# Three splits and a copy change places in the queues of ScalarE and VectorE of a fused Perceiver layer

## The chip, the core and the metric

The kernel runs on one core of a Trainium2 chip. Its time is device microseconds (us) of one launch; the kernel before took 1712.28 us, the median of 3 runs (1712.24 to 1717.71). Lower is better. Five engines work side by side and each takes its own instructions strictly in order: TensorE (PE in the rows), VectorE (DVE), ScalarE (ACT), GpSimd (POOL) and SyncE (SP, which here issues the DMAs). They meet only at semaphores.

## The reference, cut to what matters

`x` is 256 x 512, the context `ctx` 25088 x 512. The layer is a cross attention of x over the context, then a self attention and a mixture of experts. The change touches the first part alone:

```
Q = layernorm(x);  q = Q Wq^T + bq;  k = ctx Wk^T + bk;  v = ctx Wv^T + bv      # 8 heads of 64
attn = softmax(q k^T / sqrt(64));  x = x + attn v
x = x + self_attention(layernorm(x));  x = x + experts(layernorm(x))
```

## The kernel before

The context is worked off in 49 chunks of 512 rows (NCH = 49). Matmuls run in float16; each float32 value is split into a high half, rounded to float16, and a low half, the rest, and a product takes three matmuls. Two operations belong to each split: ACT copies the value to float16 (the high half) and DVE or POOL subtracts that from the value (the low half).

K and V of a chunk are two groups (h = 0 is K, h = 1 is V) of seven block products each, a Strassen-like scheme: the units M1, M5, M6, M2, M7, M3, M4, 12 matmuls each (`unit`, L1067 to L1102). A unit reads the seven blocks of the split context, `ctx_s`: four blocks are the context itself, and the others are sums of blocks that POOL forms in `t_f`. Units add up in four half banks of `ps_proj`. The results are blocks C11, C22, C12 and C21; C11 lies in bank 0 for both K and V. ACT writes a block's high half (`block_highs`), DVE its low half (`block_lows`), and only after that the bank may be filled again. So M1, the first unit of each group, which starts bank 0 anew, waits for C11's low half of the group before it: `block_low` at least 4g - 3 (L1082). This is also the first unit of a step, and there it waits for the split context as well (L1080).

The work is a software pipeline over steps c (`cross_steps`). Step c does the softmax of chunk c, the projections of chunk c + 1 and the context split of chunk c + 2. A step has two halves, h = 0 and 1, and each half two of the four head pairs g = 2h and 2h + 1. For a head pair PE forms scores in `ps_s` (L1116); DVE takes their maximum (`maxima`, L777 and L784); ACT exponentiates (`exps`, L519, four instructions); ACT writes the high half of the probabilities (`p_highs`, L530) and DVE the low half (`p_lows`, L790); DMA turns them; PE multiplies them with V (L1134). `ps_s` holds one head pair, so the scores of the next wait for `exp_done`. DVE's `step_max` (L834) follows the maxima of a half's second head pair. `add_c22` (L825) completes C22, and the unit M4 waits for it (L1091).

The context split of chunk c + 2 lies in ACT's `ctx_highs` (L439 in half 0; L442 and twice L445 in half 1) and POOL's `ctx_parts` (L366 in half 0; L372 and twice L376 in half 1, the low halves). When POOL has done the last L376, `ctx_low` lets M1 of the next step start. Before half 0 POOL forms the block sums (L349 to L354), and `rescale` (L403 to L408) scales the running sums.

The order of each engine's queue is written out by hand in `step` of that engine; steps with all three chunks in range are c = 0 to 46.

Of the kernel before, what the change touches and what calls it, by code (L numbers as in the profile page):

```python
# [56 lines left out]
def exists(c, n, count=NCH):  # L57

    return not isinstance(c, int) or 0 <= c + n < count


def after(c, n, least=0):

    return not isinstance(c, int) or c + n >= least


def back(c, u, lag, per=NG):

    return (c, u - lag) if u >= lag else (c - 1, u - lag + per)


def layer(nc, x, ctxt, wq, wk, wv, bv, cols, w_in, wg, w1, w2, w3, out):
    with ExitStack() as ctx:
# [138 lines left out]
        def bank(h, role):  # L212

            return (0, (1, 2)[h], (2, 1)[h], 3)[role]

        def out_k(kk, odd, i, j):

            return k_s[odd][kk][:, 2 * i:2 * i + 2, j * HC:(j + 1) * HC]

        def out_v(kk, odd, i, j):  # L220

            return v_s[odd][kk][:, 2 * j:2 * j + 2, i * QUARTER:(i + 1) * QUARTER]


        C11, C22, C12, C21 = (0, 0, 0), (3, 1, 1), (2, 0, 1), (1, 1, 0)

        def half_bank(n):

            return ps_proj[:, n, :].rearrange("p (t k) -> p t k", t=2)
# [196 lines left out]
        def _(act):  # L426
# [8 lines left out]
            def ctx_highs(k, odd, half):  # L435

                if half == 0:
                    act.wait_ge(ctx_loaded[odd], 8 * k + (16 - 8 * odd))
                    act.activation(ctx_s[odd][0][:, 0:2, :, :].rearrange("p b t k -> p (b t) k"), ctx_f[odd][:, :, 0:QUARTER],  # L439
                                   ACT.Copy).then_inc(ctx_high, 1)  # L440
                else:
                    act.activation(ctx_s[odd][0][:, 2, :, :], ctx_f[odd][:, 2:4, QUARTER:CH], ACT.Copy).then_inc(ctx_high, 1)  # L442
                    for n in range(2):
                        act.wait_ge(t_sum, 4 * k + 3 + n)
                        act.activation(ctx_s[odd][0][:, 3 + 2 * n:5 + 2 * n, :, :], t_f[:, 2 * n:2 * n + 2, :, :],  # L445
                                       ACT.Copy).then_inc(t_high, 1)
# [17 lines left out]
            def seed(k, h):  # L464

                g = 2 * k + h
                act.wait_ge(unit_done, UNITS * g + 1)
                if not isinstance(k, int) or g >= 1:
                    act.wait_ge(block_low, 4 * g - 1)
                a, b = half_bank(bank(h, 0)), half_bank(bank(h, 1))  # L470
                if h == 0:
                    for t in range(2):
                        ins = act.activation(b[:, t, :], a[:, t, :], ACT.Identity, bias=bk_s[:, 2 + t:3 + t])
                else:
                    ins = act.activation(b, a, ACT.Copy)
                ins.then_inc(seeded, 1)
# [9 lines left out]
            def block_highs(k, h, which, odd):  # L486

                role, i, j = which
                g, ps = 2 * k + h, half_bank(bank(h, role))
                if which == C22:  # L490
                    act.wait_ge(c22_done, g + 1)
                else:
                    act.wait_ge(unit_done, UNITS * g + {C11: 4, C12: 6, C21: 7}[which])
                if h == 1:
                    ins = act.activation(out_v(0, odd, i, j), ps, ACT.Copy)  # L495
                elif which == C11:
                    for t in range(2):
                        ins = act.activation(out_k(0, odd, i, j)[:, t, :], ps[:, t, :], ACT.Identity, bias=bk_s[:, t:t + 1])
                else:
                    ins = act.activation(out_k(0, odd, i, j), ps, ACT.Copy)  # L500
                ins.then_inc(block_high, 1)
# [9 lines left out]
            def exps(c, g, odd):  # L511

                act.wait_ge(nmax_done, NG * c + g + 1)
                if g % 2 == 0 and after(c, -2):
                    act.wait_ge(scaled, 2 * (c - 2) + g // 2 + 1)
                for b in range(2):
                    for r in range(2):
                        col = 4 * g + 2 * b + r
                        ins = act.activation(prob[:, g % 2, (2 * b + r) * HC:(2 * b + r + 1) * HC],  # L519
                                             ps_s[:, b, r * HC:(r + 1) * HC], ACT.Exp, bias=nmax[odd][:, col:col + 1],  # L520
                                             scale=LOGIT_SCALE, accum_out=lsum[odd][:, col:col + 1])
                ins.then_inc(exp_done, 1)
# [9 lines left out]
            def step(c, odd):  # L532
                for h in range(2):
                    if exists(c, h):
                        block_highs(c + h, 1 - h, C21, odd if h == 0 else 1 - odd)
                    if exists(c, 1):
                        seed(c + 1, h)
                    pc, pg = back(c, 2 * h, 1)
                    if exists(pc, 0):
                        p_highs(pc, pg)  # L540
                    if exists(c, -1) and h == 0:
                        alphas(c - 1, 1)
                    if exists(c, 0) and h == 1:
                        alphas(c, 0)
                    if exists(c, 1):
                        copy_m5(c + 1, h)
                    if exists(c, 0):
                        exps(c, 2 * h, odd)
                    if exists(c, 0):
                        p_highs(c, 2 * h)  # L550
                    if exists(c, 1):
                        block_highs(c + 1, h, C11, 1 - odd)
                    if exists(c, 2):
                        ctx_highs(c + 2, odd, h)
                    if exists(c, 1):
                        for which in (C22, C12):
                            block_highs(c + 1, h, which, 1 - odd)
                    if exists(c, 0):
                        exps(c, 2 * h + 1, odd)
# [83 lines left out]
        def _(dve):  # L643
# [149 lines left out]
            def block_lows(k, h, which, odd):  # L793

                role, i, j = which
                g, ps = 2 * k + h, half_bank(bank(h, role))
                dve.wait_ge(block_high, 4 * g + 1 + (C11, C22, C12, C21).index(which))
                if h == 1:
                    ins = dve.tensor_tensor(out_v(1, odd, i, j), ps, out_v(0, odd, i, j), ALU.subtract)  # L799
                elif which == C11:  # L800
                    for t in range(2):
                        ins = dve.scalar_tensor_tensor(out=out_k(1, odd, i, j)[:, t, :], in0=ps[:, t, :], scalar=bk_s[:, t:t + 1],  # L802
                                                       in1=out_k(0, odd, i, j)[:, t, :], op0=ALU.add, op1=ALU.subtract)
                else:
                    ins = dve.tensor_tensor(out_k(1, odd, i, j), ps, out_k(0, odd, i, j), ALU.subtract)
                ins.then_inc(block_low, 1)
# [48 lines left out]
            def step(c, odd):  # L855
                for h in range(2):
                    if exists(c, h):
                        block_lows(c + h, 1 - h, C21, odd if h == 0 else 1 - odd)
                    if exists(c, 0):
                        maxima(c, 2 * h, odd)  # L860
                    if isinstance(c, int) and c == -1 and h == 1:
                        split_q()
                    pc, pg = back(c, 2 * h, 1)
                    if exists(pc, 0):
                        p_lows(pc, pg)
                    if exists(c, 1):
                        add_u4(c + 1, h)
                    if exists(c, -1):
                        add_o(c - 1, h)
                    if exists(c, 0):  # L870
                        p_lows(c, 2 * h)
                    if exists(c, 1):
                        add_c22(c + 1, h)
                        block_lows(c + 1, h, C11, 1 - odd)
                    if exists(c, 0):
                        maxima(c, 2 * h + 1, odd)
                        step_max(c, h, odd)
                    if exists(c, 1):
                        for which in (C22, C12):
                            block_lows(c + 1, h, which, 1 - odd)  # L880
                    if isinstance(c, int) and c == -1 and h == 1:
                        tisa_scores()

            cross_steps(dve, step)


# [413 lines left out]
```

## Time and profile before

| | |
|---|---|
| median of 3 runs | 1712.28 us |
| the profiled execution | 1712.28 us, of which the span is 1710.6 us |
| PE busy | 1566.7 us, 92% of the span |
| DVE busy | 1420.7 us, 83% |
| ACT busy | 1272.2 us, 74% |
| POOL busy | 792.5 us, 46% |
| chain that ended last, by engine | PE 32%, ACT 21%, DVE 19%, issue 15%, POOL 11% |

Busy is the time in which an engine has an instruction at work, of one execution. The chain is followed back from the last instruction, at each step to what released it. A share of busy time is an average over stages; the cross attention fills about 67 to 1365 us of the span, and there the steps repeat almost alike.

### The profile page before, as it was taken

The page shows a single profiled execution, that of the slowest core. Times are in us where ns is not written, and L with a number is a line of the kernel's source. Part 1 is how long each engine was busy: PE and PEld are TensorE (multiplying, and loading weights), DVE is VectorE, ACT ScalarE, POOL GpSimd, SP SyncE. Part 2 cuts the span into 40 slices and gives each one's busy share as a digit, 9 for nine tenths or more (in the row PEclk, how much of TensorE's full clock was granted, in tenths as well). Part 3 has the DMA queues.
Part 4 walks back from the last instruction along what each step waited for, and adds up shares of the span by engine and source line. Part 5 has one row for each costly group of instructions (what it writes and reads, how often), then busy time and mean ns, then how long its engine had stood idle before and what let it go on. Part 6 is the DMA issues. An engine that isn't in the chain of part 4 may idle for free.

```text
span 1710.6 us, 47409 instructions
## 1 busy us (share of the span) xinstructions
PE 1566.7 (92%) x17740; PEld 1273.3 (74%) x17740; DVE 1420.7 (83%) x1868; ACT 1272.2 (74%) x3075; POOL 792.5 (46%) x696
## 2 busy tenths in 40 slices
PE   3999999999999999999999999999999597999998
PEld 2777778777787787777877778778778365777776
DVE  8589888998888898988899888988988646776765
ACT  3588888888888888888888888888888534655554
POOL 5365665655656556566565565655654100000000
PEclk9999999999999999999999999999999675999999
DMA  4156445444454454544544445445455670455551
GB/s 166 45 106 137 121 102 133 107 126 123 104 140 102 120 131 102 135 122 101 134 106 125 124 103 141 101 119 132 104 134 112 149 234 1 151 219 187 212 191 50
DMA packets 442403, 216.03 MB, mean 126 GB/s; under 512 B 416736, under 2 KB 422880, under 8 KB 435568
## 3 DMA queue, kind: packets, MB, share of 16 engines
q1 hardware_dynamic: 442064, 215.07, 46.8%
q8 instruction: 34, 0.56, 0.1%
q10 hardware_dynamic: 288, 0.27, 0.1%
q14 instruction: 17, 0.14, 0.0%
HBM read 111.96 MB, written 0.56 MB: 66 GB/s over the span
## 4 chain that ended last, share of the span: by engine, by line
PE 32%; ACT 21%; DVE 19%; issue 15%; POOL 11%; DMA 1%; ACTq 0%; DVEq 0%; SPq 0%; POOLq 0%
ACT prob L519 14%; PE ps_proj L1099 10%; PE ps_proj L1234 9%; POOL ctx_s L376 8%; DVE cmax L777 8%; PE ps_o L1257 4%; DVE nmax L784 4%; PE ps_s L1116 4%; ACT p_s L530 3%; POOL ctx_s L372 3%; DVE k_s L802 2%; DVE ps_proj L825 2%; ACT ctx_s L442 2%; PE ps_s L1190 1%; PE ps_proj L1170 1%
## 5 line engine op out<-in xcount | busy, mean ns | idle before, releaser
L1099 PE MATMUL ps_proj<-ctx_s,wk_s 128*128 128x256 f16 x4116 | 496.8, 274 | 91.1 <-POOL ctx_s L376 65.2
L1099 PEld LDWEIGHTS ps_proj<-ctx_s,wk_s 128*128 128x128 f16 x4116 | 382.3, 98 | 175.9 <-issue 99.9
L1099 PE MATMUL ps_proj<-wv_s,ctx_s 128*128 128x256 f16 x4116 | 489.8, 273 | 0.0
L519 ACT ACTIVATE prob<-ps_s,nmax 128x256 f32<-128x256 f32 x784 | 360.3, 473 | 101.6 <-DVE nmax L784 101.0
L1099 PEld LDWEIGHTS ps_proj<-wv_s,ctx_s 128*128 128x128 f16 x4116 | 388.2, 98 | 62.8 <-issue 19.4
L790 DVE SCALAR_TENSOR_TENSOR p_s<-prob,p_s 128x1024 f16<-128x1024 f32 x196 | 243.7, 1243 | 80.7 <-ACT p_s L530 80.7
L777 DVE TENSOR_REDUCE cmax<-ps_s 128x4 f32<-128x1024 f32 x196 | 238.6, 1217 | 36.6 <-PE ps_s L1116 36.6
L372 POOL TENSOR_TENSOR ctx_s<-ctx_f,ctx_s 128x512 f16<-128x512 f32 x48 | 57.3, 1193 | 380.1 <-ACT ctx_s L442 380.1
L530 ACT ACTIVATE p_s<-prob 128x1024 f16<-128x1024 f32 x196 | 207.5, 1059 | 6.6
L376 POOL TENSOR_TENSOR ctx_s<-t_f,ctx_s 128x1024 f16<-128x1024 f32 x96 | 202.0, 2123 | 0.0
L1234 PE MATMUL ps_proj<-x_s,wsp 128*128 128x256 f16 x1536 | 179.9, 274 | 4.2 <-issue 3.2
L1134 PE MATMUL ps_o<-v_s,pt_s 128*128 128x64 f16 x4704 | 172.2, 194 | 8.5 <-DMA pt_s<-p_s 8.4
L1116 PE MATMUL ps_s<-k_s,q_s 64*128 64x256 f16 x2352 | 164.3, 273 | 15.5 <-ACT prob L519 15.5
L1234 PEld LDWEIGHTS ps_proj<-x_s,wsp 128*128 128x128 f16 x1536 | 151.0, 98 | 36.3 <-issue 3.5
L1134 PEld LDWEIGHTS ps_o<-v_s,pt_s 128*128 128x128 f16 x4704 | 166.1, 99 | 15.2 <-DMA pt_s<-p_s 10.7
L366 POOL TENSOR_TENSOR ctx_s<-ctx_f,ctx_s 128x1024 f16<-128x1024 f32 x48 | 102.1, 2127 | 134.0 <-ACT ctx_s L439 134.0
L519 ACT ACTIVATION_READ_ACCUMULATOR prob<-ps_s,nmax 128x1 f32 x784 | 160.8, 205 | 0.0
L1116 PEld LDWEIGHTS ps_s<-k_s,q_s 64*128 64x128 f16 x2352 | 99.3, 95 | 69.3 <-issue 30.5
L834 DVE TENSOR_TENSOR dmax<-nmax 128x8 f32<-128x8 f32 x98 | 143.3, 1462 | 3.4
L905 DVE SCALAR_TENSOR_TENSOR wsp<-wst,wsp 128x1024 f16<-128x1024 f32 x96 | 114.6, 1222 | 31.2 <-ACT wsp L585 31.2
L799 DVE TENSOR_TENSOR v_s<-ps_proj,v_s 128x512 f16<-128x512 f32 x196 | 125.4, 678 | 3.0 <-ACT v_s L495 3.0
L784 DVE SCALAR_TENSOR_TENSOR nmax<-cmax,nmax 128x4 f32<-128x4 f32 x196 | 106.2, 542 | 10.4
(156 smaller groups left out, 2016.4 us busy)
## 6 DMA issues: line engine op xcount, KB each, us to landing
ctx_f<-ctxt_dram SPq DMA_DIRECT2D x49, 1024.0 KB, 5.1
wst<-w_dram SPq DMA_DIRECT2D x96, 512.0 KB, 4.9
pt_s<-p_s SPq DMA_TRANSPOSE x392, 2.7
w_in_sb<-w_in_dram SPq DMA_DIRECT2D x1, 3072.0 KB, 10.9
tisa<-tisa_scores SPq DMA_DIRECT2D x3, 1024.0 KB, 14.5
w_f<-wk_dram SPq DMA_DIRECT2D x1, 1024.0 KB, 7.7
w_f<-wv_dram SPq DMA_DIRECT2D x1, 1024.0 KB, 11.5
w_f<-wq_dram SPq DMA_DIRECT2D x1, 1024.0 KB, 13.3
```

The source lines that it names most:

```text
L376: pool.tensor_tensor(out=low[:, 3 + 2 * n:5 + 2 * n, :, :], in0=t_f[:, 2 * n:2 * n + 2, :, :], in1=high[:, 3 + 2 * n:5 + 2 * n, :, :], op= ...
L519: ins = act.activation(prob[:, g % 2, (2 * b + r) * HC:(2 * b + r + 1) * HC], ps_s[:, b, r * HC:(r + 1) * HC], ACT.Exp, bias=nmax[odd][:, ...
L530: act.activation(p_s[:, g % 2, 0, :], prob[:, g % 2, :], ACT.Copy, scale=P_SCALE).then_inc(p_high, 1)
L777: dve.tensor_reduce(cmax[:, g % 2, :], ps_s[:, :, :].rearrange("p b (r k) -> p (b r) k", r=2), AX, ALU.max).then_inc(cmax_done, 1)
L784: dve.scalar_tensor_tensor(out=nmax[odd][:, 4 * g:4 * g + 4], in0=cmax[:, g % 2, :], scalar=-LOGIT_SCALE, in1=nmax[1 - odd][:, 4 * g:4 * g ...
L790: dve.scalar_tensor_tensor(out=p_s[:, g % 2, 1, :], in0=prob[:, g % 2, :], scalar=P_SCALE, in1=p_s[:, g % 2, 0, :], op0=ALU.mult, op1=ALU. ...
L799: ins = dve.tensor_tensor(out_v(1, odd, i, j), ps, out_v(0, odd, i, j), ALU.subtract)
L834: dve.tensor_tensor(dmax[:, cols], nmax[odd][:, cols], nmax[1 - odd][:, cols], ALU.subtract).then_inc(dmax_done, 1)
L1099: ins = pe.matmul(ps_proj[:, bank(h, role), sub * QUARTER:(sub + 1) * QUARTER], lhsT, rhs, start=(fresh and sub == 0 and t == 0 and i == 0 ...
L1116: ins = pe.matmul(ps_s[:, head, r * HC:(r + 1) * HC], q_s[a][rows, g, r * P:(r + 1) * P], k_s[odd][b][rows, g, r * HC:(r + 1) * HC], start ...
L1134: ins = pe.matmul(ps_o[:, vg // 2, col:col + DK], pt_s[:, vg, a, 4 * head + tile, :], v_s[vodd][b][:, tile, u * DK:(u + 1) * DK], start=(i ...
L1234: ins = pe.matmul(ps_proj[:, u % 2, m * T:(m + 1) * T], wsp[a][:, (u // 2) % 2, m, col:col + P], x_s[b][:, t, :], start=(t == 0 and k == 0 ...
```

## The change

In ACT's queue `ctx_highs` now comes directly behind the exponentials of the half's first head pair. Before, it stood behind that pair's `p_highs` and C11's high half; both come after it now. In DVE's queue the low half of C11 moves from behind `add_c22` to behind the maxima of the half's second head pair and `step_max`, where it leads C22 and C12. No instruction is added or removed; PE, POOL and SP keep their order.

```diff
@@ ACT, step(c, odd) @@
                     if exists(c, 0):
                         exps(c, 2 * h, odd)
+                    if exists(c, 2):
+                        ctx_highs(c + 2, odd, h)
                     if exists(c, 0):
                         p_highs(c, 2 * h)
                     if exists(c, 1):
-                        block_highs(c + 1, h, C11, 1 - odd)
-                    if exists(c, 2):
-                        ctx_highs(c + 2, odd, h)
-                    if exists(c, 1):
-                        for which in (C22, C12):
+                        for which in (C11, C22, C12):
                             block_highs(c + 1, h, which, 1 - odd)
                     if exists(c, 0):
                         exps(c, 2 * h + 1, odd)
@@ DVE, step(c, odd) @@
                     if exists(c, 1):
                         add_c22(c + 1, h)
-                        block_lows(c + 1, h, C11, 1 - odd)
                     if exists(c, 0):
                         maxima(c, 2 * h + 1, odd)
                         step_max(c, h, odd)
                     if exists(c, 1):
-                        for which in (C22, C12):
+                        for which in (C11, C22, C12):
                             block_lows(c + 1, h, which, 1 - odd)
```

DVE's queue in half 0 of a step before; L802 is the low half of C11 of K, L805 those of C22, C12 and, from the next half, C21:

```order
L790 SCALAR_TENSOR_TENSOR p_s<-prob,p_s 128x1024
L825 TENSOR_TENSOR ps_proj<-ps_proj,m_f 128x512
L802 SCALAR_TENSOR_TENSOR k_s<-ps_proj,bk_s,k_s 128x256 x2
L777 TENSOR_REDUCE cmax<-ps_s 128x4
L784 SCALAR_TENSOR_TENSOR nmax<-cmax,nmax 128x4
L834 TENSOR_TENSOR dmax<-nmax 128x8
L805 TENSOR_TENSOR k_s<-ps_proj,k_s 128x2x256 x3
```

And the same place of the changed kernel, whose lines stand two lower:

```order
L788 SCALAR_TENSOR_TENSOR p_s<-prob,p_s 128x1024
L823 TENSOR_TENSOR ps_proj<-ps_proj,m_f 128x512
L775 TENSOR_REDUCE cmax<-ps_s 128x4
L782 SCALAR_TENSOR_TENSOR nmax<-cmax,nmax 128x4
L832 TENSOR_TENSOR dmax<-nmax 128x8
L800 SCALAR_TENSOR_TENSOR k_s<-ps_proj,bk_s,k_s 128x256 x2
L803 TENSOR_TENSOR k_s<-ps_proj,k_s 128x2x256 x3
```

The pair for C11 moved behind three instructions. In half 1 it is the same with one instruction, L799, on V.

ACT's queue in half 1 of a step before, from the exponentials of head pair 2 to those of pair 3; L530 is `p_highs`, the first L495 the high half of C11 of V:

```order
L519 ACTIVATE prob,lsum<-ps_s,nmax 128x256 x4
L530 ACTIVATE p_s<-prob 128x1024
L495 ACTIVATE v_s<-ps_proj 128x2x256
L442 ACTIVATE ctx_s<-ctx_f 128x512
L445 ACTIVATE ctx_s<-t_f 128x1024 x2
L495 ACTIVATE v_s<-ps_proj 128x2x256 x2
L519 ACTIVATE prob,lsum<-ps_s,nmax 128x256 x4
```

And of the changed kernel:

```order
L519 ACTIVATE prob,lsum<-ps_s,nmax 128x256 x4
L442 ACTIVATE ctx_s<-ctx_f 128x512
L445 ACTIVATE ctx_s<-t_f 128x1024 x2
L530 ACTIVATE p_s<-prob 128x1024
L495 ACTIVATE v_s<-ps_proj 128x2x256 x3
L519 ACTIVATE prob,lsum<-ps_s,nmax 128x256 x4
```

The three context copies moved ahead of `p_highs`; in half 0 one copy, L439, did.

## Rows read from the trace of the kernel before

**Rows 1.** Waits, whole span: engine, line, releaser; us in total, times, longest

```profile
PE ps_proj L1099 <- POOL ctx_s L376: 65.2, 47, 1.4
```

**Rows 2.** Timeline, PE, one step; start, us, then idle before and its releaser

```profile
595.68 1.48 PE L1099 MATMUL ps_proj<-ctx_s,wk_s 128*128 128x256 f16 x12 [1.41 <-POOL ctx_s L376]
...
608.03 1.47 PE L1099 MATMUL ps_proj<-wv_s,ctx_s 128*128 128x256 f16 x12
609.68 0.83 PE L1116 MATMUL ps_s<-k_s,q_s 64*128 64x256 f16 x12 [0.17 <-ACT prob L519]
...
619.27 1.48 PE L1099 MATMUL ps_proj<-wv_s,ctx_s 128*128 128x256 f16 x12
622.14 1.48 PE L1099 MATMUL ps_proj<-ctx_s,wk_s 128*128 128x256 f16 x12 [1.40 <-POOL ctx_s L376]
```

**Rows 3.** Timeline, POOL, the same step

```profile
599.26 1.26 POOL L352 TENSOR_TENSOR t_f<-ctx_f,t_f 128x512 f32<-128x512 f32 x1
...
605.44 2.13 POOL L366 TENSOR_TENSOR ctx_s<-ctx_f,ctx_s 128x1024 f16<-128x1024 f32 x1 [2.63 <-ACT ctx_s L439]
...
607.69 1.04 POOL L405 TENSOR_TENSOR o_acc<-o_acc,alpha 128x512 f32<-128x512 f32 x1
...
616.63 1.20 POOL L372 TENSOR_TENSOR ctx_s<-ctx_f,ctx_s 128x512 f16<-128x512 f32 x1 [7.74 <-ACT ctx_s L442]
617.79 4.21 POOL L376 TENSOR_TENSOR ctx_s<-t_f,ctx_s 128x1024 f16<-128x1024 f32 x2
```

**Rows 4.** Timeline, ACT, the same step

```profile
604.31 1.05 ACT L439 ACTIVATE ctx_s<-ctx_f 128x1024 f16<-128x1024 f32 x1
...
612.46 0.47 ACT L519 ACTIVATE prob<-ps_s,nmax 128x256 f32<-128x256 f32 x1
...
614.49 1.06 ACT L530 ACTIVATE p_s<-prob 128x1024 f16<-128x1024 f32 x1
...
615.93 0.62 ACT L442 ACTIVATE ctx_s<-ctx_f 128x512 f16<-128x512 f32 x1
616.45 1.99 ACT L445 ACTIVATE ctx_s<-t_f 128x1024 f16<-128x1024 f32 x2
```

**Rows 5.** Timeline, DVE, the same step

```profile
599.31 1.23 DVE L784 SCALAR_TENSOR_TENSOR nmax<-cmax,nmax 128x4 f32<-128x4 f32 x1
...
604.86 0.69 DVE L825 TENSOR_TENSOR ps_proj<-ps_proj,m_f 128x512 f32<-128x512 f32 x1
605.47 0.87 DVE L802 SCALAR_TENSOR_TENSOR k_s<-ps_proj,bk_s,k_s 128x256 f16<-128x256 f32 x2
606.25 1.21 DVE L777 TENSOR_REDUCE cmax<-ps_s 128x4 f32<-128x1024 f32 x1
607.50 0.16 DVE L784 SCALAR_TENSOR_TENSOR nmax<-cmax,nmax 128x4 f32<-128x4 f32 x1
607.70 1.06 DVE L834 TENSOR_TENSOR dmax<-nmax 128x8 f32<-128x8 f32 x1
...
615.58 1.23 DVE L790 SCALAR_TENSOR_TENSOR p_s<-prob,p_s 128x1024 f16<-128x1024 f32 x1 [0.94 <-ACT p_s L530]
...
617.33 0.68 DVE L799 TENSOR_TENSOR v_s<-ps_proj,v_s 128x512 f16<-128x512 f32 x1
...
619.97 2.05 DVE L834 TENSOR_TENSOR dmax<-nmax 128x8 f32<-128x8 f32 x1
```

**Rows 6.** Timeline of the two first steps, DVE and POOL

```profile
78.59 0.17 DVE L834 TENSOR_TENSOR dmax<-nmax 128x8 f32<-128x8 f32 x1
...
96.53 2.37 DVE L790 SCALAR_TENSOR_TENSOR p_s<-prob,p_s 128x1024 f16<-128x1024 f32 x1
96.55 1.27 POOL L352 TENSOR_TENSOR t_f<-ctx_f,t_f 128x512 f32<-128x512 f32 x1
```

**Rows 7.** DMA issues of the page: kind, count, us to landing

```profile
pt_s<-p_s SPq DMA_TRANSPOSE x392, 2.7
```

**Rows 8.** Windows: us, busy (instructions) by engine, PE clock, DMA

```profile
600.00:1200.00 600.00, 565.27 (x7091) 471.32 (x7090) 537.36 (x683) 500.77 (x1272) 359.75 (x315) 1.00 0.48 120
```

## The prediction

> **What bounds the kernel now.** I read the waits over the whole span first, then one step of the timeline engine by engine; times "at s" are us from the start of the step's first unit M1 (595.68 in the trace). The reader is to see three things.
>
> First, PE is the engine at the limit, and one wait per step stands in its queue: 47 times it waits for POOL's last context low half, 65.2 us in all, about 1.4 us a time [rows 1]. The step from 595.68 to 622.14 lasts 26.46 us [rows 2]; 600 us of the loop hold 565 us of PE work at granted clock 1.00, that is 2.4 GHz [rows 8]. At most the 1.4 us wait and the 0.17 us before the third scores could come out of a step.
>
> Second, that wait is the end of a chain: ACT's L442, POOL's L372, twice L376, then M1 [rows 3, 4]. The exponentials that start at 612.46 give way to L530 at 614.49, and L442 starts only at 615.93: 1.44 us later, about what PE waits. Taking L442 ahead of the two operations is worth just the wait, if nothing else becomes late.
>
> Third, DVE and POOL shut each other out at times. The nmax at 599.31 works on 4 columns and took 1.23 us, ending with POOL's L352 [rows 3, 5], where the same instruction took 0.16 at 607.50; dmax took 1.06 beside L405 and 2.05 us beside the second L376, against 0.17 us at 78.59 [rows 3, 5, 6]. And one of the 1024-column `p_lows`, asked for as L352 ran (96.55 to 97.82), took 2.37 instead of 1.23: it ended 1.08 us after L352 [rows 5, 6]. I take it that a DVE instruction with two SBUF inputs waits for the POOL instruction that is running, and gets in before the next.
>
> **The change, half 0.** In its first part nothing moved. With M1 released later (below) POOL's sums lie about 1.7 us earlier against M1, so L352 (at s 3.6 to 4.8 before) is over when nmax is asked for at s 3.63; L354 behind it ends near 4.35. nmax ends at 4.4 instead of 4.86, the exponentials start at 4.45 and take 2.0. Then the moved copy L439 starts at 6.4 and holds ACT for 0.95, so `p_highs` starts at 7.35 and `p_lows` is asked for 1.1 us later (614.49 to 615.58 [rows 4, 5]), at 8.45. But POOL's L366 starts 1.13 us after L439 (604.31 to 605.44) and runs 2.13: 7.55 to 9.7. `p_lows` waits for it and ends 1.08 behind, at 10.75; before it ended at 9.27. So a copy of 1 us costs 1.5 us: 0.95 on ACT and 1.2 behind POOL, less the earlier exponentials.
>
> Behind it on DVE: `add_c22` 0.6 (604.86 to 605.47), maxima 1.25 (606.25 to 607.50), nmax 0.15: done at 12.7 [rows 5]. Before, C11's low half stood between, 0.8 us; now it comes next. `step_max` took 1.06 beside L405; POOL now does its L405 in the gap before, so I take 0.1, and then C11's low half, 0.87, ends at 13.7. M1 of the V group waits for exactly this half block and starts at 13.8, 0.1 behind its semaphore. Before it started at 12.35 (608.03 [rows 2]), right behind M4, since C11's low half had ended at 10.66 (605.47 + 0.87). A slack of 1.7 us has turned into a wait: +1.45 us. M4, held by `add_c22` to 11.4 instead of 11.04, is covered by this.
>
> **The change, half 1.** From M1 to the exponentials of head pair 2 took 4.43 us (608.03 to 612.46), 0.17 of it the scores' wait [rows 2, 4], which goes; so they start at 18.05, and end at 20.1 (2.03 us later). Now L442 and both L445 come first: L442 at 20.1, L445s from 20.6, `p_highs` at 22.5, `p_lows` asked for at 23.6. POOL's L372 starts 0.7 behind L442 at 20.8, lasts 1.1, and the first L376 runs from 21.9 to 24.0. `p_lows` falls into it, runs 24.0 to 25.1, and holds the second L376 off: 25.1 to 27.2. So the last context low half ends not 1.4 us earlier but 0.9 us later (26.32 before). `add_c22` ends at 25.7, so M4, which PE reaches 11.24 behind the group's M1 (608.03 to 619.27) at 25.0, waits 0.7; maxima end at 26.9, and nmax waits for the second L376, to 27.2. `step_max` falls beside `rescale`'s L405 as in half 0 before: 1.0. C11's low half 0.7 (617.33), semaphore 0.1: the next step's M1 starts at 29.0. Scores of head pair 0 follow M1 by 1.4 us, when the exponentials of pair 3 (27.25 to 29.3) are done. So the removed wait of 1.4 is replaced by two: about 1.1 us before M1 of V (M4 ends near 12.7) and about 1.9 before M1 of the next step (M4 ends near 27.1).
>
> **The rest.** `p_lows` of pair 0 comes 1.5 us later and of pair 2 about 4 us; their transposes land in 2.7 us [rows 7], and PE uses them two head pairs later (`PV_LAG`), where a head pair takes a quarter of a step, some 7 us: covered. The load of a context chunk follows the same `p_lows` on SP, again 1.5 us late, with most of a step to spare. C22's and C12's low halves come 1.3 us after C11's, before the seeds, which follow M1 (1.48 us [rows 2]), and M5, which comes after the scores, need their banks. If that cover were gone, they would add tenths per step.
>
> **The sum.** 29.0 - 26.46 = 2.54 us in each of 47 steps: 119 us. In step 47 no context is left to split; only half 0 is late, by 0.1 + 0.87 + 0.1 behind nmax, 0.7 us. The prologue step, where ACT writes a context copy ahead of C11's high half, may lose 1 us. Total +121. The profiled execution took 1712.28 us, the same as the median of the three runs, so the forecast is **1833 us**. My durations add overlaps of 0.05 to 0.1 at a dozen joints, so a step may lie anywhere from 28.3 to 29.4: 1800 to 1852 us.
>
> The Trainium skill bears on the third reading. SBUF — State Buffer, section "Who interferes with whom", says that VectorE's second input goes through a port shared with GpSimd, an exclusive lock for the whole instruction, and that an operation with one input in PSUM does not contend. By that rule all three collisions above block as the rows suggest, and C11's low half (one input in `ps_proj`) never does. One row of a `p_lows` held up is thin evidence for it; the rule lowers the chance of the first rival, and moves no term of the sum.
>
> **The rivals.** (1) *`p_lows` is not held by POOL.* For it: the 1.23 at 615.58 is the common size; against it: that one ran before L372, with POOL idle [rows 3, 5], and the one that met a running instruction took 2.37. Then `p_lows` ends at 9.65 in half 0, M1 of V starts at 12.7, and in half 1 `p_lows` runs 22.5 to 23.7, nmax ends at 25.7 to 26.2, depending on L405, and M1 starts at 26.6 to 27.2: +0.15 to +0.75 a step, 1719 to 1748 us.
> (2) *`p_lows` of pair 2 misses the gap.* It is asked for 0.4 us before the first L376 ends. If it comes behind that, it waits for the second, to 26.1, and ends at 27.2; `add_c22` 0.6, maxima 1.25, nmax 0.15, then dmax without L405 0.1, C11 0.7 and 0.1: M1 at 30.1, +3.6 a step, 1883 us.
> (3) *Faster: C11's low half gates nothing.* If the maxima and dmax on DVE run early enough that C11's low half ends before PE comes (within 12.35 and 25.0), the moved copies do what the chain says and the 65.2 us of waits go: 1647 us. It decides at 1.4 us of delay on DVE per half. For it speaks only that DVE idles 0.94 before `p_lows` [rows 5]; against it that nmax alone ended at 11.98 before (607.50 + 0.16), and C11's 0.87 behind it already makes 12.9.
> (4) *PE's clock.* The gaps grow from 1.4 to about 3.7 us a step. Granted clock was 1.00 with the present gaps [rows 8]; a fall to 1.2 GHz would put the time far above any case here. I give it 1 in 50.
>
> **How the numbers follow.** Forecast mechanism 0.69 (1800 to 1852), rival 1 0.10, rival 2 0.12, rival 3 0.05, rival 4 0.02, something of no effect 0.02. The range takes in half of rival 1's upper end, or a lock that acts in one place only, and the lower part of rival 2 in steps that now hit and now miss the gap: 1745 to 1875. Within 0.3% of 1712 us, which is about what can be told from no change, I put 0.04 (the lowest end of rival 1 and no effect), faster 0.06, slower 0.90.
>
> **What would show it.** PE's wait for L376 is gone or small, and PE waits for C11's low halves (L800 and L797 in the new file) before both M1, 1.1 and 1.9 us, and for `add_c22` before M4; `p_lows` averages about 1.6 us or more instead of 1.23, POOL's L376 about 2.6 instead of 2.1; dmax is short in half 0; the step lasts 29.0 us. It is wrong if `p_lows` stays at 1.23 beside POOL, if M1 starts at once, or if M1 waits for something else on DVE or ACT.

## The result: slower, by about a third of what was forecast

| | before | changed |
|---|---|---|
| median | 1714.99 us (4 runs) | 1758.26 us (4 runs) |
| profiled span | 1710.6 us | 1757.6 us |
| one step, M1 to M1 | 26.46 us | 27.37 us |

The ratio is 1.0247, 95% interval 1.022 to 1.0274: slower, and inside the range of 1745 to 1875 us, but 43 us where 121 were forecast, 119 of them in the steps. (The medians of before differ by 1 to 3 us between groups of runs; each ratio is taken against the runs beside it.)

The waits of the changed kernel over the whole span, with the columns of [rows 1]:

```profile
PE ps_proj L1096 <- DVE k_s L800: 40.5, 47, 0.9
PE ps_proj L1096 <- DVE v_s L797: 35.3, 47, 0.9
...
PE ps_proj L1096 <- DVE ps_proj L823: 26.9, 48, 1.3
```

The 47 waits for L376 are gone, as forecast, and in their place stand 47 waits for C11's low half of K, 47 for that of V, and 48 for `add_c22`. They sum to 102.7 us where 65.2 stood. These are the three waits that the prediction named; each is shorter than it said.

One step of PE, as in [rows 2]; it starts at 614.14 and the next at 641.51:

```profile
614.14 1.48 PE L1096 MATMUL ps_proj<-ctx_s,wk_s 128*128 128x256 f16 x12 [0.74 <-DVE v_s L797]
...
627.57 1.48 PE L1096 MATMUL ps_proj<-wv_s,ctx_s 128*128 128x256 f16 x12 [0.87 <-DVE k_s L800]
...
639.28 1.48 PE L1096 MATMUL ps_proj<-wv_s,ctx_s 128*128 128x256 f16 x12 [0.54 <-DVE ps_proj L823]
...
641.51 1.48 PE L1096 MATMUL ps_proj<-ctx_s,wk_s 128*128 128x256 f16 x12 [0.74 <-DVE v_s L797]
```

Its DVE, against [rows 5]; the first `p_lows` is that of pair 0, the second that of pair 2:

```profile
617.78 0.48 DVE L782 SCALAR_TENSOR_TENSOR nmax<-cmax,nmax 128x4 f32<-128x4 f32 x1
...
622.24 2.31 DVE L788 SCALAR_TENSOR_TENSOR p_s<-prob,p_s 128x1024 f16<-128x1024 f32 x1 [1.47 <-ACT p_s L530]
...
637.08 1.54 DVE L788 SCALAR_TENSOR_TENSOR p_s<-prob,p_s 128x1024 f16<-128x1024 f32 x1 [3.12 <-ACT p_s L530]
...
640.38 0.24 DVE L782 SCALAR_TENSOR_TENSOR nmax<-cmax,nmax 128x4 f32<-128x4 f32 x1
640.65 0.17 DVE L832 TENSOR_TENSOR dmax<-nmax 128x8 f32<-128x8 f32 x1
```

Its POOL, against [rows 3]:

```profile
616.97 1.27 POOL L352 TENSOR_TENSOR t_f<-ctx_f,t_f 128x512 f32<-128x512 f32 x1
...
621.34 2.13 POOL L366 TENSOR_TENSOR ctx_s<-ctx_f,ctx_s 128x1024 f16<-128x1024 f32 x1 [0.81 <-ACT ctx_s L439]
...
635.40 5.20 POOL L376 TENSOR_TENSOR ctx_s<-t_f,ctx_s 128x1024 f16<-128x1024 f32 x2
640.56 0.21 POOL L403 TENSOR_TENSOR l_acc<-l_acc,alpha 128x8 f32<-128x8 f32 x1
640.72 1.04 POOL L405 TENSOR_TENSOR o_acc<-o_acc,alpha 128x512 f32<-128x512 f32 x1
```

Both collisions are there. `p_lows` of pair 0 is asked for at 622.24, inside L366 (621.34 to 623.47), and ends at 624.55, 1.08 us behind it. `p_lows` of pair 2 is asked for at 637.08, inside the first L376, and the two L376 take 5.20 us where they took 4.21. But in the last row of DVE dmax took 0.17 us, where the prediction had priced it at 1.0.

And its ACT, against [rows 4]:

```profile
618.39 0.47 ACT L519 ACTIVATE prob<-ps_s,nmax 128x256 f32<-128x256 f32 x1
...
620.20 1.07 ACT L439 ACTIVATE ctx_s<-ctx_f 128x1024 f16<-128x1024 f32 x1
...
631.76 0.47 ACT L519 ACTIVATE prob<-ps_s,nmax 128x256 f32<-128x256 f32 x1
...
633.56 0.65 ACT L442 ACTIVATE ctx_s<-ctx_f 128x512 f16<-128x512 f32 x1
```

The copies start 1.81 and 1.80 us after the exponentials, not 2.0. What stood there before, `p_highs`, waits for the exponentials' semaphore and started 2.03 us after them in half 1 [rows 4] and 1.96 after them in half 0; the copies need nothing of them.

### The profile page after: what moved, and what is told of

Its sections match the earlier page's. It is cut to its first block, busy times and chain, and to the rows that moved or that the text cites. A ratio compares the mean times of both kernels' runs of the same rounds, so it can differ in the third digit from the quotient of the medians.

```text
span 1757.6 us, 47409 instructions
## 1 busy us (share of the span) xinstructions
PE 1581.0 (90%) x17740; PEld 1278.4 (73%) x17740; DVE 1311.5 (75%) x1868; ACT 1264.4 (72%) x3075; POOL 884.1 (50%) x696
## 4 chain that ended last, share of the span: by engine, by line
PE 36%; DVE 24%; ACT 21%; issue 16%; DMA 1%; DVEq 1%; ACTq 0%; POOL 0%; SPq 0%
PE ps_proj L1096 14%; ACT prob L519 10%; DVE cmax L775 9%; PE ps_proj L1231 9%; ACT p_s L530 6%; ACT ctx_s L445 4%; PE ps_s L1113 4%; PE ps_o L1254 4%; DVE ps_proj L823 4%; DVE nmax L782 2%; DVE v_s L797 2%; DVE k_s L800 2%; DVE p_s L788 2%; PE ps_s L1187 1%; PE ps_proj L1167 1%
## 5 line engine op out<-in xcount | busy, mean ns | idle before, releaser
L1096 PE MATMUL ps_proj<-wv_s,ctx_s 128*128 128x256 f16 x4116 | 491.9, 273 | 66.1 <-DVE k_s L800 40.5
L1096 PE MATMUL ps_proj<-ctx_s,wk_s 128*128 128x256 f16 x4116 | 494.6, 274 | 62.6 <-DVE v_s L797 35.3
L1096 PEld LDWEIGHTS ps_proj<-wv_s,ctx_s 128*128 128x128 f16 x4116 | 384.2, 98 | 147.0 <-DVE k_s L800 53.6
L788 DVE SCALAR_TENSOR_TENSOR p_s<-prob,p_s 128x1024 f16<-128x1024 f32 x196 | 305.1, 1557 | 224.6 <-ACT p_s L530 224.6
L372 POOL TENSOR_TENSOR ctx_s<-ctx_f,ctx_s 128x512 f16<-128x512 f32 x48 | 55.6, 1157 | 415.9 <-ACT ctx_s L442 415.9
L376 POOL TENSOR_TENSOR ctx_s<-t_f,ctx_s 128x1024 f16<-128x1024 f32 x96 | 248.6, 2613 | 0.0
L530 ACT ACTIVATE p_s<-prob 128x1024 f16<-128x1024 f32 x196 | 207.7, 1060 | 0.2
L1131 PE MATMUL ps_o<-v_s,pt_s 128*128 128x64 f16 x4704 | 172.6, 194 | 11.7 <-DMA pt_s<-p_s 11.7
L495 ACT ACTIVATE v_s<-ps_proj 128x512 f16<-128x512 f32 x196 | 113.1, 602 | 89.7 <-DVE ps_proj L823 83.7
L500 ACT ACTIVATE k_s<-ps_proj 128x512 f16<-128x512 f32 x147 | 83.2, 599 | 110.2 <-DVE ps_proj L823 108.7
L366 POOL TENSOR_TENSOR ctx_s<-ctx_f,ctx_s 128x1024 f16<-128x1024 f32 x48 | 103.3, 2152 | 49.6 <-ACT ctx_s L439 49.6
```

The source lines that it names most:

```text
L376: pool.tensor_tensor(out=low[:, 3 + 2 * n:5 + 2 * n, :, :], in0=t_f[:, 2 * n:2 * n + 2, :, :], in1=high[:, 3 + 2 * n:5 + 2 * n, :, :], op= ...
L530: act.activation(p_s[:, g % 2, 0, :], prob[:, g % 2, :], ACT.Copy, scale=P_SCALE).then_inc(p_high, 1)
L788: dve.scalar_tensor_tensor(out=p_s[:, g % 2, 1, :], in0=prob[:, g % 2, :], scalar=P_SCALE, in1=p_s[:, g % 2, 0, :], op0=ALU.mult, op1=ALU. ...
L1096: ins = pe.matmul(ps_proj[:, bank(h, role), sub * QUARTER:(sub + 1) * QUARTER], lhsT, rhs, start=(fresh and sub == 0 and t == 0 and i == 0 ...
L1131: ins = pe.matmul(ps_o[:, vg // 2, col:col + DK], pt_s[:, vg, a, 4 * head + tile, :], v_s[vodd][b][:, tile, u * DK:(u + 1) * DK], start=(i ...
```

## The experiments

The theory after the result: the forecast mechanism is right, and the step is 1.6 us shorter than forecast mainly because dmax in half 1 gets in before L405. The rivals: the two halves, or the two engines' parts, do something else than the prediction said, and 43 us is a chance sum. Each ratio below is against the kernel before, run beside it.

**VectorE's part alone.** Edit, on the kernel before:

```diff
                         add_c22(c + 1, h)
-                        block_lows(c + 1, h, C11, 1 - odd)
                     if exists(c, 0):
                         maxima(c, 2 * h + 1, odd)
                         step_max(c, h, odd)
                     if exists(c, 1):
-                        for which in (C22, C12):
+                        for which in (C11, C22, C12):
```

> VectorE's part of the change alone, ScalarE's queue as before. My theory (C11's low half behind the maxima and step_max makes both M1 wait): M1 of V starts 0.8 to 1.6 us later than the 12.35 us of before, and in half 1 dmax falls beside a context low half of GpSimd again, so that C11's low half ends behind it: 27.5 to 28.5 us a step against 26.46, about 1760 to 1806 us. Rival (the moved low halves hide, and the loss came from ScalarE's part): 1712 us, no wait for C11's low half before M1.

Measured: 1755.81 us, ratio 1.022 (1.019 to 1.025), just under the range given. Late low halves of C11 gate M1 without any help from ACT, so the rival falls. But the place was half right: only M1 of the next step waits, by 1.94 us, since dmax, held 2.05 us by the second L376, now stands ahead of C11's low half there; M1 of V shows no wait. Two of its steps on PE:

```profile
614.01 2.67 PE L1098 MATMUL ps_proj<-ctx_s,wk_s 128*128 128x256 f16 x12 [1.94 <-DVE v_s L799]
...
642.34 1.48 PE L1098 MATMUL ps_proj<-ctx_s,wk_s 128*128 128x256 f16 x12 [1.93 <-DVE v_s L799]
```

The plain step of this kernel lasts 26.87 us (642.34 to 669.21), +0.41. About every third step, as the one from 614.01, lasts 28.33: behind the wait the same 12 matmuls take 2.67 instead of 1.48 us, PE being at its lower clock level (granted 0.52 from 614 to 617 us, 1.00 from 642 to 645). 0.41 x 47 is 19 us of the 40 lost; the rest comes with the longer steps, 13 of them and the first.

**ScalarE's part alone.** Edit, on the kernel before:

```diff
+                    if exists(c, 2):
+                        ctx_highs(c + 2, odd, h)
                     if exists(c, 0):
                         p_highs(c, 2 * h)
                     if exists(c, 1):
-                        block_highs(c + 1, h, C11, 1 - odd)
-                    if exists(c, 2):
-                        ctx_highs(c + 2, odd, h)
-                    if exists(c, 1):
-                        for which in (C22, C12):
+                        for which in (C11, C22, C12):
```

> ScalarE's part of the change alone, VectorE's queue as before. My theory: p_lows comes 0.9 us later on ScalarE and is then held by GpSimd's L366 and by the first L376 (it averages about 1.55 us, not 1.22), M1 waits for no C11 low half, but the scores of the next pair wait for late exponentials: about 27.3 us a step, 1740 to 1775 us. Rival (the chain of the waits table is all that counts and VectorE's part did the harm): the 1.4 us wait is gone and the time is about 1650 to 1665 us.

Measured: 1833.65 us, ratio 1.0686 (1.0655 to 1.0716), far above the range. `p_lows` averages 1.56 us as expected, and no M1 waits for C11. The scores wait, in both halves:

```profile
604.34 0.83 PE L1114 MATMUL ps_s<-k_s,q_s 64*128 64x256 f16 x12 [1.27 <-ACT prob L519]
...
619.15 0.83 PE L1114 MATMUL ps_s<-k_s,q_s 64*128 64x256 f16 x12 [1.57 <-ACT prob L519]
```

The step is 29.0 us. With C11's low half ahead of the maxima, all that is late reaches nmax and the exponentials, and these are then the bound. So the two hunks do not add: 118 us for ACT's, 40 for DVE's, 43 for both. DVE's hunk takes C11's low half out of the softmax's chain, 0.8 us in half 0 and 0.6 in half 1, and with that pays back most of ACT's loss. The prediction left these times out of the chain in its sum, but named the hunk only as a cost and did not say what it gives.

**Half 0 alone, half 1 alone.** Edit, for half 0 on ACT; DVE is branched in the same way, and half 1 alone has the test turned round:

```diff
+                    if h == 0:    # the changed order
+                        ctx_highs(c + 2, odd, h)
+                        p_highs(c, 2 * h)
+                        for which in (C11, C22, C12):
+                            block_highs(c + 1, h, which, 1 - odd)
+                    else:         # the order of before
+                        p_highs(c, 2 * h)
+                        block_highs(c + 1, h, C11, 1 - odd)
+                        ctx_highs(c + 2, odd, h)
+                        for which in (C22, C12):
+                            block_highs(c + 1, h, which, 1 - odd)
```

> The whole change in half 0 only, half 1 as before. My theory: M1 of V starts 1.1 us later (13.4 instead of 12.35 us), the exponentials of pair 2 0.85 us later, and the wait for the context low halves stays at the end of the step: +0.85 us a step, 1752 us. Rival (half 1 is where the loss is made): 1712 us.

> The whole change in half 1 only, half 0 as before. In the changed kernel M1 of V to the next M1 took 13.94 us (613.43 minus 600.20 plus the rest of the step); behind a V group that starts at 12.35 as before this gives 26.3 us a step: 1700 to 1712 us, the gain of the earlier context split and the new wait for C11's low half cancel. Rival (half 1 carries the loss of the changed kernel): 1750 us or more.

Measured: half 0 alone 1789.44 us, ratio 1.0423 (1.0388 to 1.0458); half 1 alone 1702.58 us, ratio 0.9932 (0.9906 to 0.9958). The second is as expected, and faster than both kernels of the case: the loss is made in half 0. The first is 37 us above what I expected. Its step:

```profile
603.44 1.48 PE L1118 MATMUL ps_proj<-ctx_s,wk_s 128*128 128x256 f16 x12 [1.40 <-POOL ctx_s L376]
...
607.07 1.24 DVE L793 SCALAR_TENSOR_TENSOR nmax<-cmax,nmax 128x4 f32<-128x4 f32 x1
...
608.42 0.48 ACT L519 ACTIVATE prob<-ps_s,nmax 128x256 f32<-128x256 f32 x1 [0.69 <-DVE nmax L793]
...
617.60 1.48 PE L1118 MATMUL ps_proj<-wv_s,ctx_s 128*128 128x256 f16 x12 [0.86 <-DVE k_s L811]
```

Nmax of pair 0 took 1.24 us here, held by POOL, and the exponentials behind it start 4.98 us after M1, where in the changed kernel they start 4.25 after it (618.39 - 614.14). M1 of V follows at 14.16 (617.60 - 603.44) against 13.43 (627.57 - 614.14): the same 0.73. The wait of 1.40 for L376 stays, since half 1 has the old order. The step is 28.06 us. So in the changed kernel the late M1 of half 1 gives something back: POOL's sums have run further by then, and nmax of pair 0 waits only for the end of L352 (616.97 to 618.24) and takes 0.48 us. It is held there too, but for less. Half 0 costs +1.60 a step by itself, half 1 gives 0.22, and both together cost +0.91.

**A nudge ahead of dmax.** Edit, on the changed kernel: a wait for nmax and a one-column memset stand before dmax in half 1, so that dmax is asked for a little later.

```diff
                         maxima(c, 2 * h + 1, odd)
+                        if h == 1:
+                            dve.wait_ge(nmax_done, NG * c + 4)
+                            dve.memset(nudge[:, :], 0.0)
                         step_max(c, h, odd)
```

> The changed kernel with one tiny memset (one column) on VectorE between nmax and step_max's dmax in half 1. My theory of the miss: in half 1 dmax is asked for 0.07 us before GpSimd's L405 and so takes 0.17 us, where I had priced it at 1.0 behind L405; a tenth of a us more on VectorE lets L405 in first, dmax takes about 1.05, C11's low half and M1 come 0.85 us later: 28.2 us a step, about 1798 us. Rival (the order of asking is not what decides, or dmax is short for another reason): the memset costs its own 0.1 us, 1758 to 1765 us.

Measured: 1819.57 us, ratio 1.0617 (1.0599 to 1.0635); 61 us above the changed kernel and 22 above what I expected. DVE, POOL and PE about the end of one step; 613.18 is the next M1:

```profile
611.12 0.24 DVE L783 SCALAR_TENSOR_TENSOR nmax<-cmax,nmax 128x4 f32<-128x4 f32 x1
611.42 0.06 DVE L877 MEMSET nudge<- 128x1 f32 x1
611.47 1.05 DVE L833 TENSOR_TENSOR dmax<-nmax 128x8 f32<-128x8 f32 x1
...
611.47 1.04 POOL L406 TENSOR_TENSOR o_acc<-o_acc,alpha 128x512 f32<-128x512 f32 x1
...
613.18 1.48 PE L1100 MATMUL ps_proj<-ctx_s,wk_s 128*128 128x256 f16 x12 [1.68 <-DVE v_s L798]
...
616.41 1.26 POOL L355 TENSOR_TENSOR t_f<-t_f,ctx_f 128x512 f32<-128x512 f32 x1
...
616.82 0.88 DVE L783 SCALAR_TENSOR_TENSOR nmax<-cmax,nmax 128x4 f32<-128x4 f32 x1
```

In the changed kernel dmax is asked for at 640.65 and POOL's L405 at 640.72, and dmax takes 0.17. Here both are asked for at 611.47 and dmax takes 1.05. The step is 28.67 us, +1.30: 0.88 is dmax, and 0.38 is nmax of pair 0, which I had not expected to move: M1 is later against POOL's sums, so nmax now waits for the last of them (0.88 us) instead of for the end of the one before it (0.48), and the exponentials start at 4.63 after M1, not 4.25. 1.30 x 47 is 61. This is close to what the prediction described, 29.0 us and 1833, and it is one operation of eight columns that makes the difference.

**POOL's split behind `p_lows` in half 0.** Edit, on the changed kernel: POOL waits for `p_lows` of pair 0 before L366, which takes away the collision of half 0 and leaves all else.

```diff
                     pool.wait_ge(t_sum, 4 * k + 4)
+                    if after(k, -2):
+                        pool.wait_ge(p_low, NG * (k - 2) + 1)
                     pool.wait_ge(ctx_high, 2 * k + 1)
```

> The changed kernel, but GpSimd waits for the low half of head pair 0's probabilities before it starts L366. My theory (p_lows is held by the GpSimd instruction that runs): p_lows of pair 0 takes 1.22 again instead of 2.31 us, M1 of V comes 0.7 us earlier, about 26.6 us a step, 1720 to 1730 us; if dmax then falls behind L405 0.8 us of it are lost again (1758). Rival (the 2.31 us are a coincidence of something else): p_lows stays at 2.3 us and the wait adds to the time, 1758 us or more.

Measured: 1725.04 us, ratio 1.007 (1.0047 to 1.0093), as expected. The two operations that collided:

```profile
608.40 1.23 DVE L790 SCALAR_TENSOR_TENSOR p_s<-prob,p_s 128x1024 f16<-128x1024 f32 x1 [1.48 <-ACT p_s L532]
...
609.79 2.13 POOL L368 TENSOR_TENSOR ctx_s<-ctx_f,ctx_s 128x1024 f16<-128x1024 f32 x1 [3.11 <-DVE p_s L790]
```

`p_lows` takes 1.23 again, and M1 of V starts 12.74 us into the step instead of 13.43. 0.69 x 47 is 32, and 33 us are gone. So of the 43 us that the change costs, 33 hang on this one collision.

**Half 1 with the copies behind `p_highs`.** Edit, on the kernel before; half 0 is not touched.

```diff
                     # on ACT, half 1 (its if clauses left out)
                     p_highs(c, 2 * h)
-                    block_highs(c + 1, h, C11, 1 - odd)
                     ctx_highs(c + 2, odd, h)
-                    for which in (C22, C12):
+                    for which in (C11, C22, C12):
                         block_highs(c + 1, h, which, 1 - odd)
                     # on DVE, half 1
                     add_c22(c + 1, h)
-                    block_lows(c + 1, h, C11, 1 - odd)
                     maxima(c, 2 * h + 1, odd)
+                    block_lows(c + 1, h, C11, 1 - odd)
                     step_max(c, h, odd)
```

> From the kernel before, half 1 only: the context copies go ahead of C11's high half but stay behind p_highs, and C11's low half goes behind the maxima but ahead of step_max. Half 0 as before. My theory: L442 comes 0.47 us earlier, p_lows meets no GpSimd instruction, C11's low half ends before PE needs the bank (25.1), the wait for the context shrinks by 0.47: 26.0 us a step, 1690 us. Rival (the exponentials' chain decides by now): 1705 to 1715 us, with new waits of the scores for exponentials.

Measured: 1713.04 us, ratio 0.9996 (0.9987 to 1.0006): nothing, where 1690 was expected. A miss, and this is why (three engines, half 1):

```profile
618.26 0.61 ACT L442 ACTIVATE ctx_s<-ctx_f 128x512 f16<-128x512 f32 x1
...
618.39 1.23 DVE L799 SCALAR_TENSOR_TENSOR p_s<-prob,p_s 128x1024 f16<-128x1024 f32 x1 [0.94 <-ACT p_s L530]
...
618.95 1.68 POOL L372 TENSOR_TENSOR ctx_s<-ctx_f,ctx_s 128x512 f16<-128x512 f32 x1 [7.26 <-ACT ctx_s L442]
```

L372 is released earlier than before, but now inside `p_lows` (618.39 to 619.62), and takes 1.68 us instead of 1.20 [rows 3]. It ends 1.01 behind `p_lows`. The 0.47 us that ACT saved is lost on POOL, and M1 still waits 1.40 for L376. The collision works in both directions.

**L442 in half 0.** Edit, on the kernel just shown: L442, which needs only the context chunk, is moved from half 1 to half 0, ahead of the exponentials of pair 1.

```diff
-                else:
+                elif half == 2:
                     act.activation(ctx_s[odd][0][:, 2, :, :], ...)   # L442
+                else:
                     for n in range(2):                               # the L445s
...
+                    if exists(c, 2) and h == 0:
+                        ctx_highs(c + 2, odd, 2)
                     if exists(c, 0):
                         exps(c, 2 * h + 1, odd)
```

> As the last, and L442 moves into half 0, into the 0.87 us for which ScalarE waits before the exponentials of pair 1, so that GpSimd does L372 in its idle time and only the two L376 hang on ScalarE in half 1. My theory: the second L376 ends at about 25.4 us, M1 at 25.5: 25.5 us a step, about 1667 us. Rival (the scores then wait for the exponentials of pair 3, or nmax for the earlier L376): 1685 us or more.

Measured: 1663.68 us, ratio 0.9705 (0.9687 to 0.9723), as expected. The step is 25.37 us:

```profile
611.24 0.17 DVE L847 TENSOR_TENSOR dmax<-nmax 128x8 f32<-128x8 f32 x1
...
611.24 1.08 POOL L405 TENSOR_TENSOR o_acc<-o_acc,alpha 128x512 f32<-128x512 f32 x1
...
620.14 4.31 POOL L376 TENSOR_TENSOR ctx_s<-t_f,ctx_s 128x1024 f16<-128x1024 f32 x2 [6.55 <-ACT ctx_s L446]
...
622.17 0.20 DVE L797 SCALAR_TENSOR_TENSOR nmax<-cmax,nmax 128x4 f32<-128x4 f32 x1
...
624.61 1.48 PE L1125 MATMUL ps_proj<-ctx_s,wk_s 128*128 128x256 f16 x12 [0.31 <-POOL ctx_s L376]
```

L372 is out of half 1, the two L376 follow ACT's copy at once, and M1 waits 0.31 for them instead of 1.40. The two first rows bear on the nudge: dmax and L405 are asked for at the same 611.24, and here dmax got in. Between 300 and 1200 us the two starts of half 0 lie within 0.01 us of each other in 36 steps of this kernel; dmax took 0.17 us in 9 of them and 1.06 in the others. With half 1 alone it was 4 of 34, in the kernel before none of 34. Where dmax started 0.06 to 0.08 us ahead of L405, it took 0.17 every time, in every kernel here.

**The same with the first L445 early.** Edit, on top (cut to the call; `ctx_highs` is divided to match): the first of the two L445 goes behind `alphas` in half 1, ahead of the exponentials of pair 2.

```diff
                         alphas(c, 0)
+                    if exists(c, 2) and h == 1:
+                        ctx_highs(c + 2, odd, 3)     # L445 with n = 0
                     if exists(c, 1):
                         copy_m5(c + 1, h)
```

> As e8_l442_half0, and the first of the two L445 moves to behind alphas in half 1, so that GpSimd does the first L376 in its idle time too. My theory: the second L376 then ends near 23.8 us, well before PE is done with M4 (25.1): the last 0.31 us of wait for the context go, about 25.1 us a step, 1650 us. Rival (the exponentials of pair 2 come 0.6 us later for the copy, and scores then wait for exponentials): 1664 us or more.

Measured: 1627.45 us, ratio 0.9495 (0.9482 to 0.9508), better than expected and the fastest kernel of this study, by 5.05% against before. A window as in [rows 8], here from 300 to 1200 us:

```profile
300.00:1200.00 900.00, 900.00 (x11396) 761.78 (x11392) 776.62 (x1095) 800.83 (x2046) 586.79 (x513) 1.00 0.51 128
```

PE is busy 900.00 of 900.00 us and a step lasts 24.70 (609.64 to 634.34), the next 24.61: no engine makes it wait any more. Before, it waited 1.40 and 0.17 us a step, 1.57 together; the step is 1.76 to 1.85 shorter. The rest is busy time: before, PE was busy 846.60 of the same 900 us, 24.9 us a step. Why that shrank by 0.2 is not shown.

**L442 in half 0 alone.** Edit, on the kernel before: only the diff of "L442 in half 0".

> The kernel before with one edit: L442 moves into half 0, ahead of the exponentials of pair 1; every other instruction keeps its place. My theory (L372 on GpSimd, 1.2 us, is what the move takes off the end of the chain, and no p_lows is pushed beside a GpSimd instruction): the second L376 ends 0.7 us earlier, 25.75 us a step, about 1680 us. Rival (the rest of e8's edits carried its gain): 1705 us or more.

Measured: 1691.26 us, ratio 0.9871 (0.9851 to 0.9891); 11 us less gain than expected. The reason is again nmax:

```profile
606.41 4.21 POOL L376 TENSOR_TENSOR ctx_s<-t_f,ctx_s 128x1024 f16<-128x1024 f32 x2 [7.25 <-ACT ctx_s L446]
...
608.52 2.12 DVE L788 SCALAR_TENSOR_TENSOR nmax<-cmax,nmax 128x4 f32<-128x4 f32 x1
...
612.66 0.83 PE L1120 MATMUL ps_s<-k_s,q_s 64*128 64x256 f16 x12 [0.42 <-ACT prob L520]
```

Nmax is asked for at 608.52, when the first L376 has just given way to the second, and waits all of it: 2.12 us for four columns. In the kernel with both edits it takes 0.20, as it comes 0.07 before that point (622.17; the first of the pair takes about 2.10 and ends at 622.24). The exponentials of pair 3 start later for it, and the next scores wait 0.42 us for them. A step is 25.96 us where 25.75 was expected; 0.21 x 47 is 10 of the 11 us.

## Why the prediction was wrong in size and right in mechanism

The sign and the mechanism held; the size was off by a factor of 2.8. That 1758 us lies inside 1745 to 1875 is luck: the forecast mechanism was given 1800 to 1852, and the range had been widened downward for rival 1 or a lock that acts in one place only, neither of which came. Times from M1 of the step, of the changed kernel against the prediction:

| | forecast | measured |
|---|---|---|
| exponentials of pair 0 | 4.45 | 4.25 |
| L439 | 6.4 | 6.06 |
| `p_lows` of pair 0 ends | 10.75 | 10.41 |
| M1 of V | 13.8 | 13.43 |
| exponentials of pair 2 | 18.05 | 17.62 |
| L442 | 20.1 | 19.42 |
| `p_lows` of pair 2 ends | 25.1 | 24.48 |
| second L376 ends | 27.2 | 26.46 |
| dmax lasts | 1.0 | 0.17 |
| next M1 | 29.0 | 27.37 |

- **The step that failed** is "`step_max` falls beside `rescale`'s L405 as in half 0 before: 1.0". Before, dmax of half 0 was asked for at 607.70 and L405 at 607.69 [rows 3, 5], and it took 1.06. In the changed kernel it is asked for 0.07 us before L405 (0.06 to 0.08 in all steps between 300 and 1200 us) and takes 0.17. That is 0.83 of the 1.63 us by which the forecast step is too long. It has a consequence in the next half 0: M1 comes sooner after POOL's sums have begun, so nmax of pair 0 is held by L352 and not, as forecast, by L354, and the exponentials start at 4.25 instead of 4.45. The nudge shows both: asked for 0.11 us behind nmax instead of 0.03, dmax takes 1.05, the exponentials start at 4.63, and the step is 28.67 us, 1.30 longer; the kernel takes 1819.57 us. Less the 0.08 us that the memset itself puts in, about 1.2 of the 1.63 us hang on this one term.
- **It should have been two cases**, 1.0 or 0.17, since the row that the price came from had a margin of 0.01 us. The prediction kept such a pair of cases for `p_lows` of pair 2, where the margin was 0.4 us, and none here. [rows 6] held a second warning, which the prediction misread: that `p_lows` was not asked for as L352 ran, but 0.02 us ahead of it (96.53 against 96.55), and was held all the same.
- **The rest**, 0.4 us: the copies start 1.81 and 1.80 us behind the exponentials where the prediction took about 2.0, which is 0.14 us in half 0 and 0.25 in half 1. No run took the copies' start by itself; it is read from the rows of ACT.
- **Over the kernel**: M1 of step 0 stands at 66.99 us against 67.36, so the prologue gained 0.4 in these two executions where a loss of 1 was forecast. M1 of step 47 stands at 1353.06 against 1309.02; the 47 steps cost 44.4 us instead of 119, 1.9 the first of them and about 0.9 each of most others. The profiled spans differ by 47.0, so the end costs 3.0 instead of 0.7. 44.4 - 0.4 + 3.0 is 47.0 against 121, 74 us apart, as 1833 and 1758 are by 75.
- **The collisions** came as forecast: `p_lows` 2.31 in half 0 and 1.54 in half 1, ending 1.08 and 1.1 behind POOL; the L376 pair 5.20 instead of 4.21. Over all calls `p_lows` averages 1.56 us and L376 2.61, where 1.6 or more and 2.6 were forecast. Taking away the one in half 0 gives back 33 us. Rival 1, that `p_lows` is not held, falls by this.
- **Rival 2**, the missed gap, did not come: `p_lows` of pair 2 was asked for at 637.08, 0.4 before the first L376 would end, as forecast, and got in between. Rival 3, that C11's low half gates nothing, falls by the 40.5 and 35.3 us of waits for it and by VectorE's part alone, which costs 2.2% without any copy moved. Rival 4, a fall of PE's clock, was not seen in the changed kernel's steps; it is seen in VectorE's part alone.
- **The waits** before both M1 are 0.87 and 0.74 where 1.1 and 1.9 were forecast, and 0.54 before M4 where 0.7 was. What was called covered (transposes, the loads, C22's and C12's low halves) makes PE wait in none of these steps; five waits for transposes, 11.7 us in all, stand in the changed kernel where five, 8.4 us in all, stood before.
- Both collisions and the blocked nmax agree with the Trainium skill, SBUF — State Buffer, section "Who interferes with whom": VectorE's second SBUF input and GpSimd share a lock that one of them holds for a whole instruction, and order of issue decides. The page is what should have warned of the dmax case: if order decides, a margin of 0.01 us is no price. At such a margin the recorded starts do not even tell who will be held: dmax took 0.17 in 9 of 36 steps with L442 in half 0 and in none of 34 before. L372's 1.68 us behind `p_lows` shows the lock held by VectorE as well.

What stays open: why M1's wait in the changed kernel leaves the clock at 1.00 where the longer one in VectorE's part alone, each third time, does not; and whether the later start of `p_highs` than of a copy is its wait for the exponentials' semaphore or something else at that place. I tried neither by itself. The semaphore is made likelier by C21's high half, which does not need the exponentials either and also starts 1.81 us behind those of pair 1 (607.70 to 609.51, kernel before).

## What to carry to other kernels

Where two engines hold each other off for a whole instruction, write down for every pair that meets which of them asks first and by how much; under about 0.1 us, carry both outcomes to the end as separate times, because one operation of eight columns was worth 41 us here by itself, and 61 with the four-column one that it moved. Moving the copy first on its engine was no gain, as it delayed the operation behind it into the other engine's work and that wait came back on PE; what paid was to move a copy that depends on nothing late into a slot where its engine's chain had slack, and let the chain stand. And parts of a reordering don't add: 118 and 40 us for the two engines' parts, 43 for both; +1.60 and -0.22 us a step for the two halves, +0.91 for both.

## What the runs showed of the hardware that was not expected

- Asked for 0.06 to 0.08 us ahead of GpSimd's operation, an 8-column VectorE operation took 0.17 us each time. Asked for within 0.01 us of it, it took 1.06 in most steps and 0.17 in some (9 of 36 with L442 in half 0).
- Four columns are held for the whole of GpSimd's operation, as a thousand are: nmax took 2.12 us behind an L376 that had just begun.
- GpSimd is held by VectorE too: L372 took 1.68 us instead of 1.20, ending 1.01 behind `p_lows`. It happens in every step of the kernel before as well: L354 took 2.21 us beside `p_lows` of pair 3, and 1.26 or 1.27 in the nudged kernel, where it starts ahead of `p_lows`.
- PE's level: in VectorE's part alone a wait of 1.94 us was followed about every third time by 12 matmuls of up to 2.7 us, which is the lower of its two levels (1.2 GHz), and 1.93 us at other times by 1.48. With waits of 1.68 in every step, the nudged kernel stayed at a granted 1.00 between 300 and 900 us. What tells the cases apart is not known from these runs.
